# A cross-attention and FFN kernel on one core: the engines' loops over the middle steps are written out with constants

## The reference, cut to what matters

```
x = x + _L0_xattn_ref(_layernorm(x), ctx, ctx, ig_kernel, ig_bias, fg_kernel, fg_bias, outnorm_weight)
x = x + _L0_ffn_ref(_layernorm(x), w_gate, w_up, w_down)
...
# attention, per head
log_D = fg_mat + ig[..., None, :]          # fg_mat from a cumulative sum of log_sigmoid(fg)
D = jnp.exp(log_D - max_log_D)
C = (q @ k^T / sqrt(DH)) * D
h = (C / (max(|C.sum(-1)|, exp(-max_log_D)) + 1e-6)) @ v
hn = (h - mean) * rsqrt(var + 1e-6) * outnorm_weight
...
# feed-forward
gate = silu(_bitlinear(x, w_gate))
up = _bitlinear(x, w_up)
return _bitlinear(gate * up, w_down)
```

## Time and profile before

| what | value |
|---|---|
| time, median of 3 runs | 690.28 us (690.03 to 692.08) |
| span of the profiled execution, first to last instruction | 685.3 us |
| what lies around the span, by these two | 5.0 us |
| PE busy | 579.8 us, 85% of the span |
| vector engine busy | 567.8 us, 83% |
| scalar engine busy | 476.5 us, 70% |
| GpSimd busy | 284.6 us, 42% |
| mean granted TensorE clock | 0.962 of full speed |

### The profile page before, as it was taken

The page is one execution under the profiler, slowest core; times in us unless marked ns, Lnnn a source line. Parts: engine busy times, 40 slices in busy tenths (PEclk is TensorE's granted clock), DMA queues, the critical chain, the costliest instruction groups (busy, mean ns, idle before and its releaser), DMA issues. The chain is left out here.

```text
span 685.3 us, 12637 instructions
## 1 busy us (share of the span) xinstructions
PE 579.8 (85%) x3568; PEld 377.8 (55%) x3630; DVE 567.8 (83%) x1518; ACT 476.5 (70%) x716; POOL 284.6 (42%) x459
## 2 busy tenths in 40 slices
PE   1824567889998999899998999799989999799996
PEld 1814555466555655476556656576537664456442
DVE  3149776889998998989899999899899889979863
ACT  1877766478866885678757885678667875865652
POOL 2015536624554444453543455444545256344200
PEclk9999756999999999999999999999999999999999
DMA  8852724101224102520242123310252031000001
GB/s 334 342 202 93 258 77 156 32 2 46 79 93 154 47 1 78 191 72 28 77 168 77 46 77 120 125 46 3 76 190 70 16 154 46 32 1 17 32 16 47
DMA packets 30753, 63.76 MB, mean 93 GB/s; under 512 B 2304, under 2 KB 18816, under 8 KB 27136
## 3 DMA queue, kind: packets, MB, share of 16 engines
q1 hardware_dynamic: 30144, 62.92, 25.4%
q10 hardware_dynamic: 576, 0.44, 0.3%
HBM read 54.84 MB, written 8.52 MB: 92 GB/s over the span
## 5 line engine op out<-in xcount | busy, mean ns | idle before, releaser
L558 PE MATMUL GU<-WQ,xqT 128*128 128x512 bf16 x977 | 240.3, 389 | 18.0 <-DVE FF L1161 15.4
L558 PEld LDWEIGHTS GU<-WQ,xqT 128*128 128x128 bf16 x1024 | 98.7, 100 | 121.5 <-DVE FF L1161 13.7
L588 PE MATMUL ACC<-WQ,FF 128*128 128x512 bf16 x497 | 115.0, 379 | 3.0 <-ACT FF L813 2.2
L794 ACT ACTIVATE FF<-GU,cgu 128x512 f32<-128x512 f32 x128 | 86.4, 688 | 24.5 <-PE GU L558 21.8
L1161 DVE TENSOR_TENSOR FF<-FF,GU 128x512 f32<-128x512 f32 x128 | 85.1, 680 | 8.5 <-ACT FF L794 5.5
L588 PEld LDWEIGHTS ACC<-WQ,FF 128*128 128x128 bf16 x512 | 49.6, 98 | 58.1 <-ACT FF L813 2.6
L802 ACT ACTIVATE FF<-FF,magic,hs 128x1024 f32<-128x1024 f32 x64 | 79.1, 1239 | 3.2 <-DVE hs L1192 3.2
L760 ACT ACTIVATE work<-AT,pb 128x128 f32<-128x128 f32 x128 | 47.9, 452 | 17.5 <-POOL pb L1450 16.4
L1457 POOL TENSOR_TENSOR work<-work,norm_bc 128x512 f32<-128x512 f32 x32 | 42.4, 1325 | 39.4 <-ACT work L760 39.4
L506 PE MATMUL AT<-vext,CT 128*128 128x129 f32 x256 | 54.1, 295 | 5.2 <-ACT gate_parts L699 3.8
L1412 POOL TENSOR_TENSOR qw<-qT,bc 128x512 f32<-128x512 f32 x32 | 46.0, 1448 | 19.6 <-DMA bc<-gate_rows 19.6
(11 more groups left out here) (116 smaller groups left out, 1187.7 us busy)
## 6 DMA issues: line engine op xcount, KB each, us to landing
bc<-gate_rows SPq DMA_DIRECT2D x8, 2048.0 KB, 7.4
xin<-in_x SPq DMA_DIRECT2D x32, 256.0 KB, 2.8
kT<-in_ctx_t SPq DMA_DIRECT2D x8, 1024.0 KB, 4.8
vext<-in_ctx SPq DMA_DIRECT2D x32, 256.0 KB, 3.4
out<-FF SPq DMA_DIRECT2D x32, 256.0 KB, 2.3
WQ<-in_w_gate SPq DMA_DIRECT2D x4, 1024.0 KB, 12.8
FF<-in_w_up SPq DMA_DIRECT2D x4, 1024.0 KB, 15.5
FF<-in_w_down SPq DMA_DIRECT2D x4, 1024.0 KB, 4.8
```

What stands on the lines that cost most here:

```text
L558: last = nc.tensor.matmul(dst, xqT[:, b, P * k:P * (k + 1)], w[:, k, 512 * j:512 * (j + 1)], start=(k == 0), stop=(k == KC - 1))
L588: last = nc.tensor.matmul(ACC[:, :], hT[:, b % 2, P * k:P * (k + 1)], WD[:, k, :], start=(k == 0), stop=(k == JT - 1))
L794: nc.scalar.activation(sg[:, j % 2, :], GU[:, 2 * (j % 2), :], ACT.Silu, scale=cgu[:, b, 0:1]).then_inc(silu_done, 1)
```

## The change

The three-part run of `iteration` is replaced on all five engines by one Python loop over all steps, so that the body of steps 2 to 6 stands five times in each engine's program, with constants. PE's two calls of `count_passed` ahead of the loop go with it; the helper adds the same increments at the next use of the bank.

```diff
-FULL, FULL_END = 2, NG - 1
...
-            for it in range(-1, FULL):
-                iteration(it)
-            with sp.Fori(FULL, FULL_END) as it:
-                iteration(it)
-            for it in range(FULL_END, NG + 2):
+            for it in range(-1, NG + 2):
                 iteration(it)
...
-            for it in range(-1, FULL):
-                iteration(it)
-            count_passed("tp", tp_out, (FULL + 1) * len(TP_ORDER) + 1)
-            count_passed("at", at_out, (FULL + 1) * len(AT_ORDER) + 1)
-            with pe.Fori(FULL, FULL_END) as it:
-                iteration(it)
-            for it in range(FULL_END, NG + 2):
+            for it in range(-1, NG + 2):
                 iteration(it)
```

## The result

| kernel | median | range | runs |
|---|---|---|---|
| before, beside it | 690.15 us | 688.69 to 692.08 | 4 |
| changed | 701.97 us | 700.02 to 708.71 | 4 |

The ratio is 1.0196, with a 95% interval of 1.0144 to 1.0248. The prediction said 686.5 us in a range of 680.5 to 690.5, so it had the sign wrong, and the result lies above its range. The profiled execution of the changed kernel took 700.02 us, its span 698.1 us against 685.3.

What follows compares the result with a forecast made beforehand. The prediction took the vector engine's stream, in its time between pieces, as the bound. Register instructions saved 5.3 us, less 0.5 lost in waits and 1.0 for code: 3.8 us off 690.3 gave 686.5 us, range 680.5 to 690.5.

Steps and rivals of the forecast that it cites:

- What bounds the kernel: In the loop rounds, the vector engine leads about 60 of 74 us; its stream's time between two pieces is the bound.
- The vector engine's register instructions: In the loop, 68 fewer vector engine instructions a round save 1.07 us a round, 5.3 us for five rounds.
- 0.5 of losses: At L1044 the vector engine waits for PE's L484, giving back 0.1 us a round, 0.5 us in all.
- The places: Behind L1111, idle of 0.40 or 0.41 us becomes 0.32 to 0.34; L1122 overlaps L970 where 0.13 us was idle.
- rival 1: At round heads, some falls of PE's granted clock vanish: three fewer give 681.4 us, one more 688.2; chance 0.20.
- rival 2: The vector engine reaches PE-led places earlier and waits there, swallowing the gain: 688.9 us; chance 0.18 shared with a no-effect case.
- The register instructions of PE, the scalar engine, GpSimd and SP I cost at nothing: Outside the vector engine, removed register instructions gain nothing; without cover, PE's would be worth up to 3 us a round.
- The argument against it: At the round heads, PE's idle hardly shrinks, since PE and the vector engine both come earlier.
- Code supply: The longer code moves about 29 more instruction packets; one in 11 exposed at 0.37 us costs 1.0 us.
- Rival 3: Nearly every added instruction packet stops a stream that leads: 10.7 us paid against 4.8 gained, 696.2 us; chance 0.12.
- The range: For the whole kernel, 680.5 to 690.5 us, leaving out most of the slower case in which nearly every packet stops a stream.

## Why the prediction was wrong, point by point

- **What bounds the kernel: right.** The vector engine's stream sets the pace. The losses found above pass through it: its pieces held up by GpSimd, its wait for the broadcast, and, behind a lower clock of PE, its wait at L1188.
- **The vector engine's register instructions: right in sum.** Forecast 5.3 us less 0.5 of losses; written out alone it gave 5.0 us. The places look as forecast: behind L1096 (L1111 of before) the idle is 0.32 us, and L1107 (L1122) overlaps L955 (L970) by 0.08. Two rows of the changed kernel, which answer to the earlier trace rows:

```profile
314.93 0.18 DVE L955 BATCH_NORM_AGGREGATE mv_a<-st_a 128x2 f32<-128x6 f32 x1
315.03 0.66 DVE L1107 BATCH_NORM_STATS2 st<-xin 128x6 f32<-128x512 f32 x1
...
344.85 0.69 DVE L1188 TENSOR_SCALAR FF<-TPB 128x1024 bf16<-128x1024 int16 x1 [0.32 <-DVE state L1096]
```

  By rounds the sum came about otherwise. In the trace with the vector engine alone written out, three of four rounds run at full clock (one before):

```profile
236.12:308.74 72.62, 67.77 (x448) 43.93 (x455) 67.14 (x186) 54.88 (x86) 34.41 (x56) 1.00 0.26 88
...
381.28:454.89 73.61, 69.40 (x447) 44.76 (x454) 67.65 (x186) 54.78 (x86) 34.62 (x56) 0.98 0.24 86
```

  A full-clock round took 72.5 to 72.9 us, hardly less than the 72.8 of before, one with a fall 73.6 against 74.5 to 75.0. So in that trace rival 1 (falls that vanish) and shorter rounds with a fall made the gain, and in the full-clock rounds most of it was swallowed as rival 2 had it. That the sum fits the forecast so well is in part luck.
- **"The register instructions of PE, the scalar engine, GpSimd and SP I cost at nothing": this step failed.** The reason given, that GpSimd is idle over half of the time and PE has cover, is right for their own progress and says nothing of what they do to others. It was treated as a gain of nothing to perhaps 3 us; a loss was not in its bounds at all. What the runs showed in its place: without its register instructions GpSimd's pieces hold up the vector engine's x_norm, `floor_n` and L1148 for 1.0 to 1.1 us each time that they meet, and SP's broadcast lands later. GpSimd's alone was 2.6% (some 18 us by its ratio), PE's 0.6%, SP's 0.3% alone and more in company. Shares do not add up: PE and the three others alone come to 3.5%, less 0.7% of the vector engine, and the full change is 2.0%.
- **PE's clock (rival 1): right as a mechanism, sized for the other side.** Falls gone were to bring up to 5.1 us, and one more fall 688.2 us. In the changed kernel the four rounds have 20.5 us at the lower level in place of 10.2, three falls' worth more, at a price that fits the 1.3 to 2.1 us given for each. The argument against it took both engines to come earlier, and the vector engine came later. It also took PE's stand of 1.77 us at the head without a fall to be as long as the others; that holds for the 1.75 us of the first head, and the other two had 2.42 and 2.50.
- **Code supply: 1.0 us forecast, nothing found.** The 0.55 us at the first L1006 behind the loop, on which the term rested, was a cost of *leaving the loop*, or at least went with it: in the changed kernel that place has 0.15 us like all others, with ten times the packets in the rounds. All eight kernels that keep the vector engine's loop have 0.55 or 0.56 us there, and none of the twelve that have it written out. Rival 3 reached the right side for the wrong reason. What the Trainium skill says of straight code in "Runtime: NRT & Kernel Launch", section "Instruction fetch mechanics", "mostly hidden", agrees with this trace: 29 packets in the four rounds, and one idle of 0.3 us without a releaser.
- **The range.** Its upper edge came from one mechanism that could make the kernel slower, with a chance of 0.12. The trace of before did speak of the real one, in L1056, which copies the same 16 columns in each round:

```profile
284.01 1.24 DVE L1056 COPY decay<-bc 128x16 f32<-128x16 f32 x1
...
431.90 0.18 DVE L1056 COPY decay<-bc 128x16 f32<-128x16 f32 x1 [0.65 <-DMA bc<-gate_rows]
```

  A length of one instruction that varies sevenfold with equal shape (1.24 and 0.18 us) is a sign of two engines that exclude each other, and a change that shifts one of them by 0.1 us can move it either way.

## What to carry to other kernels

Where the same instruction is several times longer at some places, find out whom it excludes or is excluded by, and ask of every change, also on the idle engine and also of changes that only take instructions away, who then starts first. A register instruction or a wait on an engine that is not the bottleneck can be a spacer that the fast engine depends on; write each engine's loop out alone before all of them together, since that told in one step what the diff and the averages hid. Where transfers start in a row behind one event, their spacing belongs to the schedule as well, and where the written out form loses a spacer, an increment that nobody waits for puts it back.

## What the hardware did that I had not expected

- GpSimd and the vector engine exclude each other for whole instructions, down to a vector piece on 128x2 elements: 0.23 us becomes 1.32 (L1148), 0.53 becomes 1.55 (x_norm), 0.16 becomes 1.25 (L1058, L1043 of the changed kernel). A difference of 0.05 to 0.1 us in GpSimd's start decides it.
- Where three transfers of 256 KB and one broadcast of 2 MB are issued 0.4 to 0.8 us apart, not 0.7 to 1.0, the last two land later: `vext`, 256 KB, after 4.9 us in place of 3.4, the broadcast after 9.1 in place of 7.4. The broadcast's issuing instruction itself takes 0.50 us in place of 0.34.
- Leaving a loop can cost the vector engine 0.4 us a little later: L1006's first execution behind the loop follows L1001 after 0.55 us (0.56 in some) in each of the eight kernels that keep the vector engine's loop, and after 0.15 us in each of the twelve that have it written out.
- With several waits ahead of a matmul it matters in these traces by 0.09 us which of them stands on the matmul and which on an instruction of its own: 0.69 or 0.78 us from the last release to the first matmul of L433.
